# Second attention of a gated transformer block: the row maxima of a step scaled and handed over in two halves instead of once

## The reference

```python
s = jnp.einsum('bhqd,bhkd->bhqk', q, k) * SCALE
p = jax.nn.softmax(s, axis=-1)
return jnp.einsum('bhqk,bhkd->bhqd', p, v)
...
ctx = _attn(qT, k.transpose(0, 2, 1, 3), v.transpose(0, 2, 1, 3))
ctx_dca = _attn(qT, k_dca.transpose(0, 2, 1, 3), v_dca.transpose(0, 2, 1, 3))
ctx = ctx + DCA_WEIGHT * ctx_dca
return ctx @ Wo + bo
```

## Time and profile before

| | us |
|---|---|
| median of 3 runs | 1051.44 (1050.54 to 1051.96) |
| the profiled execution, its own time | 1050.54 |
| its span | 1049.2 |
| PE busy | 931.9 (89%) |
| DVE busy | 701.8 (67%) |
| ACT busy | 531.1 (51%) |
| POOL busy | 301.4 (29%) |

### The profile page before, as it was taken

How to read it: one execution, slowest core, us unless ns; L and a number is a source line. 1 busy time by engine, 2 the same in 40 slices (tenths; PEclk the granted TensorE clock), 3 DMA queues, 4 the chain that set the end, 5 groups by cost and what they waited for, 6 DMA issues and landing times.

```text
span 1049.2 us, 14813 instructions
## 1 busy us (share of the span) xinstructions
PE 931.9 (89%) x4790; PEld 666.9 (64%) x4790; DVE 701.8 (67%) x1829; ACT 531.1 (51%) x1346; POOL 301.4 (29%) x284
## 2 busy tenths in 40 slices
PE   7878789999999999999999989879689898979667
PEld 3323334567999999888987767655355555545455
DVE  5899894235676657677676454667877855576764
ACT  4665672035777767666753344356356643123331
POOL 3767693112111112145101333325232100010210
PEclk9888999999999999999999999999699999989789
DMA  9500001010111125323102445412100004210201
GB/s 364 233 0 0 1 0 51 0 31 31 47 46 46 46 66 212 136 71 97 46 1 86 156 143 189 151 55 71 51 1 1 2 1 146 75 46 31 88 1 41
DMA packets 28499, 75.00 MB, mean 71 GB/s; under 512 B 4092, under 2 KB 5382, under 8 KB 27656
## 3 DMA queue, kind: packets, MB, share of 16 engines
q1 hardware_dynamic: 24344, 63.81, 17.9%
q0 software_dynamic: 3072, 8.39, 2.5%
q10 hardware_dynamic: 1008, 1.86, 0.6%
HBM read 52.03 MB, written 22.02 MB: 71 GB/s over the span
## 4 chain that ended last, share of the span: by engine, by line
PE 65%; DVE 14%; ACT 4%; issue 3%; POOL 1%; DVEq 0%; ACTq 0%; POOLq 0%
PE psum L1071 5%; PE psum L2203 5%; PE psum L1290 5%; PE psum L1279 5%; PE psum L1804 5%; PE psum L1259 5%; PE psum L927 4%; PE psum L1270 3%; PE psum L1098 2%; PE psum L938 2%; PE psum L1818 2%; PE psum L2222 2%; PE psum L2466 2%; PE psum L2824 2%; DVE arena L2501 2%
## 5 line engine op out<-in xcount | busy, mean ns | idle before, releaser
L1169 POOL TENSOR_TENSOR arena<-arena,mhalf 128x8 f32<-128x8 f32 x32 | 53.4, 1670 | 232.8 <-DVE arena L1149 232.8
L1394 DVE SCALAR_TENSOR_TENSOR X<-psum,arena,X 128x256 f32<-128x256 f32 x128 | 56.0, 479 | 71.2 <-PE psum L1290 68.4
L455 POOL TENSOR_TENSOR arena<-arena 128x512 f32<-128x512 f32 x64 | 82.4, 1312 | 6.2 <-DVE arena L855 3.8
L1333 ACT ACTIVATE arena<-psum,arena 128x256 f32<-128x256 f32 x128 | 71.4, 567 | 20.0 <-DVE arena L1372 17.7
L855 DVE TENSOR_TENSOR_SCAN arena<-psum,arena 128x512 f32<-128x512 f32 x64 | 74.7, 1209 | 9.0 <-ACT psum L711 7.9
L2485 ACT ACTIVATE arena<-psum,arena 128x240 f32<-128x240 f32 x128 | 57.2, 462 | 35.7 <-DVE arena L2506 24.9
L1804 PE MATMUL psum<-arena 128*128 x248 | 65.6, 387 | 10.7 <-DVE arena L1899 8.7
L545 PE MATMUL psum<-arena,ident 128*128 128x512 f32 x128 | 68.1, 657 | 0.1
L1290 PE MATMUL psum<-arena 128*128 128x256 f32 x256 | 65.9, 380 | 1.2 <-DVE X L1394 1.1
L1279 PE MATMUL psum<-arena 128*128 128x256 f32 x256 | 65.8, 380 | 0.0
L1259 PE MATMUL psum<-arena 128*128 128x256 f32 x256 | 65.8, 380 | 0.0
(11 more groups left out here) (367 smaller groups left out, 2217.8 us busy)
## 6 DMA issues: line engine op xcount, KB each, us to landing
arena<-in_w SPq DMA_DIRECT2D x32, 384.0 KB
tokens<-arena SPq DMA_DIRECT2D x2, 4096.0 KB, 22.7
arena<-tokens SPq DMA_DIRECT2D x32, 256.0 KB
results<-arena SPq DMA_DIRECT2D x32, 256.0 KB
arena<-in_moe SPq DMA_DIRECT2D x17, 384.0 KB, 3.1
arena<-in_moe SPq DMA_DIRECT2D x4, 1536.0 KB, 6.9
arena<-in_w SPq DMA_DIRECT2D x2, 1024.0 KB, 6.7
arena<-in_gu SPq DMA_DIRECT2D x1, 1280.0 KB, 7.2
```

The source lines that it names most:

```text
L455: nc.gpsimd.tensor_tensor(m.HC[:, v, :], m.Hs[:, v, :], m.Cs[:, s % 2, :], ALU.mult).then_inc(*tick("HC", s, c))
L1333: e = nc.scalar.activation(m.Pr[:, w, j, :], bank[w][:, j * S:(j + 1) * S], ACT.Exp, bias=m.nb[:, w, j:j + 1], scale=m.rr[:, u // 2 % 3, 1 ...
```

## The change

The subtraction and the scaling move into the loop over the halves. Each works on one half (two blocks) as soon as the maxima of that half are known, and raises `a2_nb` for that half. On ACT the wait for `a2_nb` moves into the loop over the four blocks, so that blocks 0 and 1 wait for half 0 alone and blocks 2 and 3 for half 1. A step of DVE has then 2 subtractions of 2 x 16 columns and 2 scalings of 2 columns, where it had one of 4 x 16 and one of 4. The scores are addressed bank by bank instead of through one view of both banks, at the same addresses. Nothing is added on PE, POOL or SP, no DMA is moved, and the result is the same.

```diff
@@ a2_exponentials_act
-    act.wait_ge(*at("a2_nb", s))
     for a in range(4):
+        act.wait_ge(*at("a2_nb", s, a // 2))
         nc.scalar.activation(pr[:, a, 0:KM], v[:, a, 0:KM], ACT.Exp, bias=m.nb[:, u, a:a + 1],
                              scale=m.SCALE, accum_out=m.sums[:, a % 2, places[a // 2], 0:1])
@@ a2_maxima_dve
-    v = k.psum[:, 2 * u * 512:(2 * u + 2) * 512].rearrange("p (a t) -> p a t", t=S)
     for e in range(2):
-        two = slice(2 * e, 2 * e + 2)
+        v, two = bank[2 * u + e].rearrange("p (a t) -> p a t", t=S), slice(2 * e, 2 * e + 2)
         dve.wait_ge(*at("a2_S", s, e))
-        nc.vector.tensor_reduce(m.mxd[:, u, two], v[:, two, KM:S], AX, ALU.max).then_inc(*tick("a2_mxd", s, e))
-        nc.vector.tensor_reduce(m.mx[:, u, two], v[:, two, 0:KM], AX, ALU.max).then_inc(*tick("a2_mx", s, e))
-    dve.wait_ge(*at("a2_mxd", s, 1))
-    nc.vector.tensor_tensor(m.Pr[:, u, :, KM:S], v[:, :, KM:S],
-                            m.mxd[:, u].unsqueeze(2).broadcast_to([P, 4, S - KM]), ALU.subtract)
-    dve.wait_ge(*at("a2_mx", s, 1))
-    nc.vector.tensor_scalar(m.nb[:, u], m.mx[:, u], -m.SCALE, None, ALU.mult).then_inc(*tick("a2_nb", s))
+        nc.vector.tensor_reduce(m.mxd[:, u, two], v[:, :, KM:S], AX, ALU.max).then_inc(*tick("a2_mxd", s, e))
+        nc.vector.tensor_reduce(m.mx[:, u, two], v[:, :, 0:KM], AX, ALU.max).then_inc(*tick("a2_mx", s, e))
+        dve.wait_ge(*at("a2_mxd", s, e))
+        nc.vector.tensor_tensor(m.Pr[:, u, two, KM:S], v[:, :, KM:S],
+                                m.mxd[:, u, two].unsqueeze(2).broadcast_to([P, 2, S - KM]), ALU.subtract)
+        dve.wait_ge(*at("a2_mx", s, e))
+        nc.vector.tensor_scalar(m.nb[:, u, two], m.mx[:, u, two], -m.SCALE, None,
+                                ALU.mult).then_inc(*tick("a2_nb", s, e))
```

More of the change, by code:

```diff
@@ L2490, in a2_maxima_dve @@
 def a2_maxima_dve(k, m, s):
-    nc, dve, at, tick, KM = k.nc, k.dve, k.s.at, k.s.tick, m.KM
+    nc, dve, at, tick, bank, KM = k.nc, k.dve, k.s.at, k.s.tick, k.bank, m.KM
     u = s % 2
```

## The result

| kernel | median, us | lowest to highest | executions |
|---|---|---|---|
| before | 1051.26 | 1050.54 to 1051.96 | 7 |
| changed | 1055.18 | 1053.62 to 1062.59 | 7 |

The ratio is 1.0053 (1.0028 to 1.008): slower, where 1050.1 with a range to 1052.4 was forecast. The ratios here go by the means rather than the medians (whose ratio is 1.0037). Two later repeats, on two chips, gave 1.0013 (0.9996 to 1.003) and 1.0011 (0.9993 to 1.0029), both with 1 inside the interval. So "between no change and 0.8% slower, about 0.1% in the repeats" is what can be said. Two executions of over 1500 us, one of them of the kernel before, are left out of all ratios and ranges.

The account below looks back on a forecast made before the run. PE was taken as busiest (89%), its waits for ACT's copy and exponentials and of L2862 capping the gain. Terms along the chain summed to 1.34 us less: 1049.2 against the profiled execution, 1050.1 against the median 1051.44; range 1048.6 to 1052.4.

Parts of the forecast that it names:

- signs that were listed as "wrong": Pass over 1.85 us, ACT waiting before block 2, L2973 idle growing as L2914's falls, clock 0.50 past 760 or none at 706.
- The likeliest case: Second attention: gains and losses along the chain sum to 1.34 us less, 1050.1 us (1049.2 to 1051.4); chance 0.50.
- case A: Start of the second attention: the clock does not fall after PE's shorter wait, 0.96 us more gain, 1049.1 us; chance 0.22.
- The term of 0.63 for step 0: Step 0, 701 to 703 us: ACT had waited 0.64 us and PE 2.69, so 0.63 us gained.
- 0.20 + 0.96 - 1.25 + 0.60: Step 2 +0.20; no clock fall 0.96 more; five passes at 726 to 771 us -0.95, gather -0.3; steps 14, 16 +0.60.
- the 0.3 for the gather at 726 us: First scaling at 726 us stands in a POOL gather ending 0.65 us later; held or not open, half charged: -0.3 us.
- 0.22 + 0.77: Steps 26 and 27: -0.19 in DVE and +0.41 from ACT's earlier start, together +0.22; step 31: ACT earlier, +0.77 us.
- Steps 18 and 19: Chain in DVE, -0.19 us; step 19's first scaling held by L3016 to 801.5, ACT starting at 801.6 as before: 0.
- step 22's +0.36: Step 22: scaling starts inside POOL's L2451, yet ACT can start at 814.75 instead of 815.11 us: +0.36 us.
- Step 8: Pass at 740 us: the longer pass costs nothing, as a POOL hold from the same DVE instruction absorbs its 0.19 us.
- Rival D: Every scaling inside any POOL instruction is held, gathers too: -0.45 us in all, 1050.5 us; chance 0.05.
- Rival C: Slow clock from 739.6 us lasts past 760 us, so matmuls L2730 take twice 3.71 us: 1053.8 us; chance 0.11.

Follow-up runs that it names:

- experiment 11: The changed kernel again, unaltered, on another chip, against the kernel before: 1052.95 us, 1.0011; its profiled execution took 1050.1 us.
- experiment 5: Changed kernel with both scalings per step replaced by one-element negating reductions (SCALE in the query mask), against the kernel before: 1051.05 us, 0.9984.
- the two of the upper group: Two single profiled executions of the unaltered changed kernel, of its slower group (1053.9 to 1056.3 us in the repeats): 1054.73 and 1054.21 us.
- experiments 9 and 10: Changed kernel with small negating reductions for scalings in steps 8, 13, 19 alone (1050.6 us, 0.9987), or in all others (1051.49 us, 0.9991), against before.
- experiment 8: Changed kernel with steps 8, 13 and 19 in the form of the kernel before, against the kernel before: 1056.7 us, 1.0041.
- the runs of 6 and 7: Changed kernel, ACT waiting for both halves, with small reductions for scalings (1054.85 us, 1.003) or no scaling (1055.27 us, 1.0024), against before.

## Why the prediction was wrong

**Right in mechanism and size.** The half of 0.86 us and the pass of 1.72; the start of ACT, 0.7 us earlier; PE's idle time for L2914, which fell by 2.5 us where 3 was said. The hand-over to ACT was misread: "0.08 to 0.17 us at other steps" behind the start of the scaling is 0.25 to 0.28 at nearly all steps of the kernel before where ACT waited for nothing else (0.19 at step 0), so ACT starts 1.04 to 1.08 us into the pass and not 0.95; since the start of before had been put too early as well, the difference stands. ACT's idle time, 31.5 us where 20 was said, is off: the holds give part of it back.

Some of the signs that were listed as "wrong" came: passes with a held scaling were longer than 1.85 us, PE's idle time for L2973 grew by 2.9 us while that for L2914 fell by 2.5, and there was no 0.50 at 706 us. The likeliest case said that the clock still falls at the start, and case A that it doesn't. Of the profiled executions under 1053 us four of five show A (that of experiment 11 has a fall at 701 us).

The term of 0.63 for step 0 measured 0.67. From there to step 18 the others with A's 0.96 make 0.20 + 0.96 - 1.25 + 0.60 = 0.51 us; measured 1.29, of which the 0.3 for the gather at 726 us is a part: the scaling inside that gather took 0.17 us, so the term was nothing. The rest of the difference was not taken apart. From step 22 to 31 the terms make 0.22 + 0.77 = 0.99; measured 0.85.

**Steps 18 and 19, "ACT starts at 801.6 as it does now: 0", failed.** With step 22's +0.36 this stretch was priced at a gain of 0.17 us; it lost 2.30. I had put the pass where it stood before and let L3016 hold it by the rest of its length. But everything ahead of it had come earlier, POOL as well as DVE. The scaling now starts 0.19 us into L3016 instead of 0.86, and is held for 1.11 us; the second half of the pass comes that much later and is held again (0.43), which has no room ahead of it. PE then waits 2.38 us where it had waited 1.79, and the clock falls. The small reduction in three steps takes this back, and its mirror brings it again.

**Step 8, "ends in a hold by POOL that starts from the same DVE instruction and absorbs it", failed by about 0.9 us.** There are two scalings now and only the last had been under the hold. The first is held for 1.91 us (1.23 before), and a whole half of the pass, 0.86 us, is still to come. Taking the holds of steps 8 and 13 away was worth 0.92 us by step 18. An absorbed wait absorbs only what stands before it.

**The rule of the Trainium skill** (SBUF — State Buffer, "Who interferes with whom") that I cited against the change is the one that decided at steps 8 and 19. The trace agrees: scalings of 2 columns were held 10 to 13 times, 5.65 to 6.23 us in all beyond their 0.16, and none of the 64 small reductions of experiment 5 took over 0.16 us. I had given the rule weight at single steps, each with the place that POOL had before. Rival D, gathers too, came out in part: in the gathers at 706 to 712 us three scalings took 0.32 to 0.38 us and one at 720.01 took 0.64, all to the end of the gather, while those that started 0.23 and 0.25 us into a gather, at 712.78 and 724.98, took 0.17.

**Rival C's mechanism was the right one for the wrong place.** A clock that falls where it had not before: I looked for it at 760 us, where it did not come. It came at 803 us in every execution of the changed kernel that was profiled, and at 842 and 927 us in the two of the upper group. My sum was made for one execution against one execution. It gave 1049.2, and the fastest of the changed kernel took 1049.47 us; that these are near is luck, since the terms above are off by 2.5 us one way and by 0.8 the other, and A came true as well. What I did not ask was how many executions would be like it: 11 of 24 in the repeats and 5 of 40 in the first measurement for the changed kernel, four in five for the one before.

**Both sides were undersized.** Reduction with ACT waiting for both halves shows 0.3% for the longer pass where I had 1.3 us (0.12%); the early start gave 5 to 8 us, against waiting for both halves, where I had 3.0 (0.63 + 0.20 + 0.60 + 0.36 + 0.41 + 0.77). The forecast lived off the difference of two sums, each too small by a third or more.

What stays open: what decides, with equal waits, whether the clock falls, and what is in the 22 executions of over 1056.32 us of the first measurement, since none like them was profiled; the stall of the last section is of a size that would fit, but it was seen in no profile of the changed kernel. That the holds, beyond the fall at 803 us, make falls of the clock more frequent is not shown either: experiments 9 and 10 have no fewer executions of a low mean clock. An earlier or later place of POOL's instructions was not tried.

## What to carry to other kernels

Before an instruction is split in two, ask what can hold it: here a scaling of two numbers, 0.17 us where nothing holds it, cost up to 1.9 us beside POOL, and splitting took the held ones from 4 to between 10 and 13, with half of the pass now standing behind the first. The split paid clearly only with the scaling folded away (negated maxima, the factor in a mask): 0.9945 and 0.9951, where neither edit alone gained. And when PE's waits of about 2 us are what a change moves, the median depends on how many executions have falls of the clock: compare several executions, not only the one that was profiled.

## What the runs showed of the hardware that was not expected

A held scaling can stand through more than the POOL instruction during which it started: at 739.24 us it stood through the end of a gather, 1.07 us of L2592 and the first L2438, 1.91 us in all, and in the kernel before the one at 741.22 us through the rest of L2592 and the first L2438. It does not always: at 799.09 us it ended with L3016, though L2451 followed at once, and at 720.01 with a gather, though L2438 followed. What tells the cases apart was not found.

The clock: with PE's waits of 2.03 and 2.13 us it fell in one execution and not in another of the same kernel at the same points.

In some profiles waits of DVE and ACT for PE end late, while POOL issues gathers back to back, and the trace names no engine of the core for it. In the experiment with the small reduction everywhere:

```profile
713.50 0.19 DVE L2499 TENSOR_REDUCE arena<-psum 128x2 f32<-128x32 f32 x1 [2.16 <-remote]
...
717.89 0.69 DVE L2674 TENSOR_TENSOR arena<-psum,arena 128x512 f32<-128x512 f32 x1 [1.94 <-remote]
717.95 0.58 ACT L2650 COPY arena<-psum 128x512 f32<-128x512 f32 x1 [6.61 <-remote]
```

The copy of ACT had waited 6.61 us. From step 3 to step 4 this execution needs some 14.4 us where the changed kernel needs 8.6. The run of experiment 8, on the same chip, has the same stall; the kernel before has a short one (2.07 us at 713.17), as have the runs of 6 and 7. What releases these waits late was not found. None of the seven profiles of the changed kernel has it, the two of the upper group included. How many of the executions of experiment 5 have it is not known, and its 0.9984 may be too high for that.
